# Decoder layer on one core: the next sequence's scores issued ahead of the output projection

## The reference

```
x = ln(x + mixer(x))                 # gated short convolutions
x = ln(x + xattn(x, ctx, masks))     # decoder layer:
      a = attention(x, x,   mask);  x = ln1(x + a)
      a = attention(x, ctx, mask);  x = ln2(x + a)
      x = ln3(x + gelu(x @ fc1 + b) @ fc2 + b)
x = ln(x + experts(x))               # one small MLP per token position
```

## Time and profile before

| | |
|---|---|
| Median of 3 runs | 538.31 us (537.59 to 538.4) |
| Profiled execution | 538.34 us |
| Its span | 536.6 us |
| Mean granted clock of TensorE | 0.951 of full speed |
| TensorE matmuls busy | 482.3 us (90%) |
| TensorE weight loads busy | 445.1 us (83%) |
| VectorE busy | 396.1 us (74%) |
| ScalarE busy | 368.5 us (69%) |
| GpSimd busy | 262.3 us (49%) |

### The profile page before, as it was taken

How to read it: one execution, slowest core, us unless ns; L and a number is a source line. 1 busy time by engine, 2 the same in 40 slices (tenths; PEclk the granted TensorE clock), 3 DMA queues, 4 the chain that set the end, 5 groups by cost and what they waited for, 6 DMA issues and landing times. The chain is left out here.

```text
span 536.6 us, 14182 instructions
## 1 busy us (share of the span) xinstructions
PE 482.3 (90%) x4662; PEld 445.1 (83%) x4662; DVE 396.1 (74%) x1882; ACT 368.5 (69%) x1394; POOL 262.3 (49%) x349
## 2 busy tenths in 40 slices
PE   3569799999998989999999999999999998989482
PEld 2558689989897989999999999999999977879372
DVE  3555678787879888887778778877777776277864
ACT  3343877868787776888878767888877675634634
POOL 0342554564748465545544445455544455243561
PEclk9878999999999999999999999999999999997665
DMA  7840000000000000400000000000000000040003
GB/s 202 257 163 2 0 2 2 2 2 2 2 2 2 1 2 1 116 3 2 2 1 2 2 3 2 2 1 3 1 2 2 2 2 1 1 161 2 2 19 79
DMA packets 15865, 14.25 MB, mean 27 GB/s; under 512 B 2865, under 2 KB 13489, under 8 KB 15665
## 3 DMA queue, kind: packets, MB, share of 16 engines
q1 hardware_dynamic: 15648, 13.08, 8.0%
q10 hardware_dynamic: 144, 0.26, 0.2%
HBM read 12.16 MB, written 1.18 MB: 25 GB/s over the span
## 5 line engine op out<-in xcount | busy, mean ns | idle before, releaser
L594 ACT ACTIVATE P<-P,at_negmax 128x128 f32<-128x128 f32 x512 | 198.9, 396 | 81.2 <-DVE at_negmax L740 81.2
L955 POOL TENSOR_TENSOR P<-P,at_inv 128x512 f32<-128x512 f32 x128 | 136.5, 1077 | 122.6 <-DVE at_inv L750 122.5
L740 DVE CUSTOM_DVE_ANT_0 P<-late_bank,maskb 128x128 f32<-128x128 f32 x512 | 111.3, 287 | 0.1
L766 DVE COPY at_PT<-late_bank 128x512 f32<-128x512 f32 x128 | 87.2, 686 | 31.0 <-PE late_bank L451 30.8
L594 ACT ACTIVATION_READ_ACCUMULATOR P<-P,at_negmax 128x1 f32 x512 | 99.9, 195 | 0.0
L451 PE MATMUL late_bank<-ident,P 128*128 128x128 f32 x512 | 76.6, 273 | 4.7 <-DVE at_negmax L740 2.3
L451 PEld LDWEIGHTS late_bank<-ident,P 128*128 128x128 f32 x512 | 59.7, 140 | 11.6 <-issue 7.3
L468 PE MATMUL late_bank<-at_k,at_q 64*128 64x128 f32 x1024 | 65.8, 278 | 0.4 <-DVE at_k L758 0.4
L468 PEld LDWEIGHTS late_bank<-at_k,at_q 64*128 64x128 f32 x1024 | 59.7, 188 | 4.4 <-issue 0.7
L483 PE MATMUL late_bank<-at_PT,V 128*64 128x128 f32 x1024 | 63.0, 276 | 0.0
L483 PEld LDWEIGHTS late_bank<-at_PT,V 128*64 128x64 f32 x1024 | 55.2, 137 | 3.9
(11 more groups left out here) (182 smaller groups left out, 1113.9 us busy)
## 6 DMA issues: line engine op xcount, KB each, us to landing
ctxT_raw<-in_ctxT SPq DMA_DIRECT2D x1, 1024.0 KB, 8.7
out<-xres SPq DMA_DIRECT2D x4, 224.0 KB, 2.5
x<-in_xT SPq DMA_DIRECT2D x1, 768.0 KB, 7.3
xres<-in_x SPq DMA_DIRECT2D x1, 768.0 KB, 12.2
tap_rows<-in_short_wT SPq DMA_DIRECT2D x3, 192.0 KB, 5.1
sa_wq_raw<-in_sa_wq SPq DMA_DIRECT2D x1, 512.0 KB, 4.9
sa_wk_raw<-in_sa_wk SPq DMA_DIRECT2D x1, 512.0 KB, 5.8
sa_wv_raw<-in_sa_wv SPq DMA_DIRECT2D x1, 512.0 KB, 8.1
```

The costliest lines, as they stand in the source:

```text
L594: last = nc.scalar.activation(P[:, n % 2, h, :], P[:, n % 2, h, :], ACT.Exp, scale=-1.0, bias=negmax[:, n % 2, h:h + 1], accum_out=total[: ...
L740: last = nc.vector.tensor_tensor_reduce(P[:, n % 2, h, :], score_bank(h), k.maskb[:, cols(n)], scale=1.0, scalar=3.0e38, op0=ALU.add, op1= ...
L766: nc.vector.tensor_copy(PT[:, HQ * g:HQ * g + HQ, :], banks[T_BANK[g % 2]][:].rearrange("p (h l) -> p h l", h=HQ)).then_inc(pt_ok, 1)
L955: nc.gpsimd.tensor_tensor(tile, tile, inv[:, n % 2, HQ * g:HQ * g + HQ].unsqueeze(2).to_broadcast([128, HQ, 128]), ALU.mult).then_inc(norm ...
```

## The change

In the loop over p on TensorE the calls `scores(p + 1)` and `out_proj(p - 2)` trade places. Nothing else differs: the waits inside the two calls, the buffers, the banks and the queues of the other engines stay as they are.

```
                 projection(p, pair_of(p, PROJECT), 1)
                 mixer_output(p, pair_of(p, OUTPUT))
+                scores(p + 1)
                 out_proj(p - 2)
-                scores(p + 1)
                 p_v(p - 1)
```

## The result

The changed kernel takes 596.16 us (median of 4 runs, 595.74 to 597.04) against 537.95 us for the kernel before (4 runs, 536.24 to 538.4). The ratio is 1.109, 95% interval 1.1067 to 1.1114: 58 us slower, where 592 was forecast, with 576 to 606 as its range. The profiled execution took 595.74 us with a span of 594.0, so the two profiled spans differ by 57.4 us.

The account below looks back on a forecast made before the run. TensorE's queue was taken as the bound before, the loop through VectorE's residual after. Terms 4.4, 5.6, 1.9, 39.5 and 2.0 sum to +53.4 us on 538.3, forecast 592 us, range 576 to 606.

Parts of the forecast that it names:

- VectorE's loop: Residual, maxima, exponentials, V copy, TensorE's v half, k copy, out_proj, next residual; about 0.5 us slack under 11.96 us before.
- The residual holds the maxima: In VectorE's in-order queue the next sequence's maxima stand behind the residual, so early scores can't start them.
- Size of the loop: Residual to residual in a steady period after the change: 14.04 us against 11.96, so +2.08 us a period.
- Which way the residual reaches the v half: Via exponentials and V copy, 5.95 us; the way via sixteen maxima and first transposes, 5.9 us, adds nothing.
- Even mixer periods 2, 4, 6: Projection products cover the k copy; period 16.80 us against 15.34, +1.46 each, 4.4 us together.
- Odd periods 3, 5, 7, 9: Longer way from v half to k copy's end; period 15.10 us against 13.70, +1.4 each, 5.6 us together.
- Periods 8, 10: Period 15.44 us against 14.49 with the x1T wait hidden, +0.95 each, 1.9 us together.
- Steady periods 11 to 29: Nineteen periods without mixer work, each +2.08 us, 39.5 us together.
- Period 30: No k copy is due; scores start where out_proj did, so only their 1.98 us is added.
- The clock rival: TensorE's idle time drops its clock to half, +7 us in each such period, four giving 620 us; chance 0.05.
- Only the k copy: TensorE waits 0.5 to 0.6 us before scores in about 20 periods, later residual absorbed: about 546 us; chance 0.06.
- TensorE stays the bound: Only order changes in TensorE's queue; the 3.6 us of x1T waits vanish, giving 534.7 us; chance 0.04.

Follow-up runs that it names:

- experiment 6: Changed kernel with the three products of v_half(p,0) issued twice from item 2 on, 0.71 us more TensorE work a period: 592.19 us.
- 8: Kernel before the change, with the three products of v_half(p,0) issued twice, 0.71 us more TensorE work a period: 555.5 us.
- experiment 1: Changed kernel with reciprocals 3 and the next sequence's maxima 0 and 1 moved ahead of the residual in VectorE's queue: 547.64 us.
- 2: Changed kernel with only the first eight heads' scores ahead of out_proj, the other eight behind it: 568.08 us.
- experiment 3: Changed kernel with p_v also moved ahead of out_proj, giving the order scores, p_v, out_proj: 684.54 us.

## Why the prediction was right, point by point

*TensorE's queue is the bound before, VectorE's loop after.* Shown from both sides by experiments 6 and 8: 0.7 us of TensorE work is free in the one and paid in the other.

*The residual holds the maxima.* Shown by experiment 1, which takes the scores out of that loop and gives back 48.5 us, and by the doses of 2 and 3: with 1.1, 2.0 and 3.9 us of products between k copy and out_proj the full-clock loop takes 13.17, 14.06 and 15.96 us.

*Size of the loop.* 14.04 us in the working, 14.06 measured. That the two agree to 0.02 us is in part luck, since four of its parts were off by up to 0.1 us and cancelled: residual to v half 5.85 instead of 5.95, k copy to scores 0.15 instead of 0.06, scores to out_proj 1.99 instead of 2.05, out_proj to residual 2.08 instead of 1.98. From v half to the end of the k copy it was 3.99, and 4.00 had been foreseen.

*Which way the residual reaches the v half.* The working led over exponentials and V copy, with the way over the sixteen maxima and the first transposes arriving at nearly the same time. In the trace both arrive within 0.1 us: the V copy ends at 346.27, and the v half starts at 346.32, 0.18 us behind the product before it, where such products follow each other after 0.12. So the wait on the V copy is 0.06 us instead of 0.1 to 0.2 and too short for the list of waits. The list has the other way: 0.79 us of the first transposes on the maxima, where I had said about 1.0. Both ways begin at the residual that holds the maxima, so the loop is the same. VectorE's wait before the residual is 3.54 us, where I had said about 3.3, and ScalarE's 4.75, where I had said about 4.7.

*The other periods.* The table holds what the two profiled traces give from residual to residual.

| Term | Forecast, us | Measured, us |
|---|---|---|
| Even mixer periods 2, 4, 6 | 4.4 | 5.1 (1.81, 1.64, 1.63) |
| Odd periods 3, 5, 7, 9 | 5.6 | 6.2 (1.33, 1.43, 1.71, 1.68) |
| Periods 8, 10 | 1.9 | 2.0 (1.05, 0.99) |
| Steady periods 11 to 29 | 39.5 | 40.0 (227.50 to 267.45) |
| Period 30 | 2.0 | 3.2 (10.65 to 13.83) |
| Period 31 | 0 | 1.1 (10.63 to 11.70) |
| Sum | 53.4 | 57.5 |

The terms are the measured growth of each period; period 2 is counted from the start of the span. The spans differ by 57.4 us; the feed-forward is the same to 0.1 us.

The largest miss is in the last two rows: 2.3 of the 4 us. I wrote that only the 1.98 us of scores is added in period 30 and nothing in 31, and that the clock stays 1.00. There TensorE lacks the units that fill the steady periods, so it waits longer for the maxima, and then its clock is found at the lower level:

```profile
485.98 0.63 PE L451 MATMUL late_bank<-ident,P 128*128 128x128 f32 x4 [1.79 <-DVE at_negmax L740]
487.21 0.50 PE L73 MATMUL late_bank<-ca_wv_hi,ctxT_hi 128*128 128x512 f32 x1 [0.60 <-ACT V L613]
...
487.80 0.63 PE L75 MATMUL late_bank<-ca_wv_hi,ctxT_lo 128*128 128x512 f32 x1
...
491.13 2.06 PE L468 MATMUL late_bank<-at_k,at_q 64*128 64x128 f32 x32
```

This is the changed kernel in period 30: waits of 1.79 and 0.60 us, and then products and transposes at half rate. From the v half to the scores it is 3.92 us, against 2.71 from the same v half to out_proj before (434.10 to 436.81). These 1.21 us and the 1.98 of the scores make up the 3.18 by which the period grew. In period 31 the same stretch takes 3.86 us, 1.15 more than those 2.71, which covers its growth of 1.07. So "the clock stays 1.00" was wrong there, and one of the prediction's own signs of being wrong, durations at half clock, did appear. The clock rival had a chance of 0.05 and a price of 7 us a period; it came in two periods at 1.2 and 1.1 us, since only a stretch of each ran at the lower level.

*The rivals that did not come.* "Only the k copy" names a real cost, 0.60 us in a steady period, but it is the smaller part: experiment 1, whose steady period is 0.67 us over the old one, takes 9.3 us more than the kernel before in all. "TensorE stays the bound" would have needed a loop that still fits under 11.96 us; it gave 534.7 us, and 596.16 was measured.

The mixer periods came out 1.4 us above the sum in all. The first of them contains 0.14 us by which the whole run was already late at the k copy of period 2 (84.92 against 84.78). The rest was not split further.

## What to carry to other kernels

Before moving a call within one engine's queue, write down the loop that it lies on: follow the released instruction through the other queues and back to the moved call, add the durations, and compare with the period. Idle time on the way is no slack if it is spent waiting for this same call. If an order is changed on the producing engine, the consuming queue has to be changed with it, and only where a wait is covered by it: here both swaps in five periods gave 0.65%, both swaps in all periods cost 1.8%, and TensorE's swap alone in all periods cost 11%.

## What was not expected of the hardware

The mean share of work did not tell whether TensorE's clock would fall. With matmuls busy 153.4 of 169.0 us and gaps of about 0.8 and 0.4 us in a period it kept 1.00. With 12.88 of 15.90 us busy it kept 1.00 in one period of experiment 3 and fell to a mean of 0.90 in others with the same work and nearly the same waits (1.38 and 0.79 us in the one, 1.48 and 0.75 in the next). In period 30 of the changed kernel it fell after waits of 1.79 and 0.60 us. With 0.7 us of products added, which made these 1.10 and 0.60 us (experiment 6), it stayed at 1.00 in period 30 and the period was 1.1 us shorter; in period 31, with the same work and the same waits, it fell all the same. What decides between two such periods, no run here shows.
